# Squaring the last stage's keys on ScalarE instead of VectorE, in a two-layer attention and expert kernel on one core

## The reference, cut to what matters

```
xn = layernorm(x)
# attention, 16 heads of 8
q, k, v = split(xn @ w_qkv);  q = elu(q) + 1;  k = elu(k) + 1
y = (q @ (k^T v)) / (q @ sum(k))
# channel mix
x_prev = xn shifted by one token within its sequence
xr = mu_r * xn + (1 - mu_r) * x_prev
xk = mu_k * xn + (1 - mu_k) * x_prev
r = sigmoid(xr @ W_r^T)
k_act = square(relu(xk @ W_k^T))
x = x + (y @ w_proj + b_proj) + r * (k_act @ W_v^T)
```

## Time and profile before

| | |
|---|---|
| Three runs, median (lowest to highest) | 349.37 us (348.57 to 349.54) |
| The profiled execution, its own time | 349.86 us |
| Its span, first to last instruction | 348.1 us |
| Granted TensorE clock, mean | 0.995 of full speed |
| Busy in the span: PE, PEld, DVE, ACT, POOL | 95%, 84%, 92%, 80%, 65% |
| The last stage, from its first kv matmul to the end | 265.3 to 348.1 us |

### The profile page before, as it was taken

The page is one execution under the profiler, slowest core; times in us unless marked ns, Lnnn a source line. Parts: engine busy times, 40 slices in busy tenths (PEclk is TensorE's granted clock), DMA queues, the critical chain, the costliest instruction groups (busy, mean ns, idle before and its releaser), DMA issues.

```text
span 348.1 us, 9108 instructions
## 1 busy us (share of the span) xinstructions
PE 330.2 (95%) x2457; PEld 293.9 (84%) x2457; DVE 318.9 (92%) x590; ACT 278.4 (80%) x805; POOL 225.3 (65%) x238
## 2 busy tenths in 40 slices
PE   7999968889999999999999899999998999999995
PEld 3878424689999999999999899999997788778875
DVE  5899999989999999999899899999979799998665
ACT  2987956977899898889788778879997788777751
POOL 3799101876776688777777768777877278874110
PEclk9999989999999999999999999999999999999999
DMA  5785595334444555664655555676452002221012
GB/s 161 213 237 141 147 427 206 107 109 137 137 138 138 140 149 162 159 189 136 178 164 161 166 161 153 160 190 161 122 144 70 1 17 54 59 57 32 30 32 60
DMA packets 47120, 47.04 MB, mean 135 GB/s; under 512 B 8528, under 2 KB 35312, under 8 KB 46816
## 3 DMA queue, kind: packets, MB, share of 16 engines
q1 hardware_dynamic: 42032, 37.23, 35.4%
q0 software_dynamic: 4320, 8.86, 10.8%
q10 hardware_dynamic: 720, 0.38, 0.5%
HBM read 32.88 MB, written 13.50 MB: 133 GB/s over the span
## 4 chain that ended last, share of the span: by engine, by line
PE 78%; DVE 15%; DMA 2%; issue 2%; ACTq 1%; ACT 0%; SPq 0%; DVEq 0%
PE banks L575 17%; PE banks L587 17%; PE banks L783 5%; PE banks L784 5%; PE banks L1106 3%; PE banks L559 2%; PE banks L1182 2%; PE banks L1135 2%; PE banks L1164 2%; PE banks L1144 2%; PE banks L868 2%; PE banks L1116 2%; PE banks L1152 2%; DVE qk_exp L408 2%; PE banks L1171 2%
## 5 line engine op out<-in xcount | busy, mean ns | idle before, releaser
L503 POOL DMA_INDIRECT xg<-xn_rows,slot_tok x71 | 85.6, 1206 | 44.7 <-DVE slot_at L1819 23.0
L604 ACT ACTIVATE xT<-banks,b1T 128x128 f32<-128x128 f32 x284 | 81.8, 378 | 12.3 <-PE banks L575 11.9
L520 POOL DMA_INDIRECT qk_exp<-expert_rows,ranki x64 | 70.2, 1097 | 18.4 <-issue 17.1
L575 PE MATMUL banks<-xgT,w 128*128 128x128 f32 x568 | 75.5, 276 | 0.2 <-ACT xgT L596 0.2
L587 PE MATMUL banks<-w_sb,xT 128*128 x568 | 75.2, 275 | 0.1
L587 PEld LDWEIGHTS banks<-w_sb,xT 128*128 128x128 f32 x568 | 69.3, 192 | 0.9 <-issue 0.3
L575 PEld LDWEIGHTS banks<-xgT,w 128*128 128x128 f32 x568 | 69.0, 192 | 0.8 <-issue 0.7
L795 DVE TENSOR_TENSOR cq<-banks,phi 128x1152 f32<-128x1152 f32 x32 | 43.2, 1350 | 5.7 <-PE banks L784 5.7
L806 DVE TENSOR_REDUCE late<-cq 128x144 f32<-128x1152 f32 (+1 forms) x32 | 45.5, 1421 | 0.1
L696 ACT CAST high<-outer 128x1152 fp32r<-128x1152 f32 x32 | 37.0, 1156 | 6.8 <-DVE outer L685 5.0
L703 DVE TENSOR_TENSOR low<-outer,high 128x1152 fp32r<-128x1152 f32 (+1 forms) x32 | 38.7, 1210 | 1.5 <-ACT high L696 1.3
(11 more groups left out here) (224 smaller groups left out, 701.3 us busy)
## 6 DMA issues: line engine op xcount, KB each, us to landing
w<-in_L_ffn_W SPq DMA_DIRECT2D x71, 256.0 KB
expert_rows<-ye SPq DMA_DIRECT2D x71, 64.0 KB
expert_rows<-x_sb SPq DMA_DIRECT2D x2, 2048.0 KB, 9.8
x_sb<-in_L_attn_x SPq DMA_DIRECT2D x8, 256.0 KB, 4.5
xn_rows<-xn_all SPq DMA_DIRECT2D x8, 256.0 KB, 4.1
w_sb<-in_L_ffn_W SPq DMA_DIRECT2D x8, 256.0 KB, 4.5
out<-outer SPq DMA_DIRECT2D x7, 256.0 KB, 2.3
xg<-xn_rows,slot_tok POOLq DMA_INDIRECT x71
```

The lines of the kernel that those rows point to most:

```text
L503: pool.indirect_dma_start(out=xg[n][:, :], out_offset=None, in_=xn_dram, in_offset=bass.IndirectOffsetOnAxis(ap=slot_tok[:, j:j + 1], axis ...
L520: pool.indirect_dma_start(out=y_moe[:, i, k, :], out_offset=None, in_=y_dram, in_offset=bass.IndirectOffsetOnAxis(ap=ranki[:, 0, k, i:i + ...
L575: last = nc.tensor.matmul(slot_bank(j)[:, c * P:(c + 1) * P], w1[n][:, c * P:(c + 1) * P], xgT[p][:, :], start=True, stop=True)
L604: last = nc.scalar.activation(hidT[p][:, c, :], slot_bank(j)[:, c * P:(c + 1) * P], ACT.Gelu_apprx_tanh, bias=b1T[:, ds(e * NC + c, 1)])
```

## The change

The hunks are of `square_keys`, `last_scalar`, `last_vector`, `group_vector` and `group_scalar`, in this order. `square_keys` moves from VectorE's queue to ScalarE's, and becomes a Square of the activation functions in place of a product of two tensors. Its waits and its semaphore stay. On ScalarE it stands behind `gate_scalar` (the tanh) and ahead of `xT2_copy` in groups 0 to 6, and behind `yT1_copy` in group 7.

```
-    def square_keys(v, g):
-        v.wait_ge(relu_ready, g + 1)
-        if from_(g, 1):
-            v.wait_ge(vf_ps, g)
-        nc.vector.tensor_tensor(k_act, k_relu, k_relu, ALU.mult).then_inc(kact_ready, 1)
+    def square_keys(act, g):
+        act.wait_ge(relu_ready, g + 1)
+        if from_(g, 1):
+            act.wait_ge(vf_ps, g)
+        nc.scalar.activation(k_act, k_relu, ACT.Square).then_inc(kact_ready, 1)
...
@@ -1247,6 +1247,7 @@
         yT1_copy(act, g - 1)
+        square_keys(act, g)
         act.wait_ge(phik_ready, NG)
...
@@ -1258,7 +1259,6 @@
         phi_q_vector(v, g)
-        square_keys(v, g)
         v.wait_ge(nd_ps, g + 1)
...
```

## The result

The changed kernel takes 350.42 us in the median of 14 runs (350.08 to 352.74), the kernel before 349.24 us beside it (348.47 to 350.38). The ratio is 1.0041, with a 95% interval of 1.0028 to 1.0055: slower by 0.4%. The time lies in the predicted range and 0.1 us from the predicted 350.5; against the kernel before on the same chips it is 1.2 to 1.4 us more, where the sum said 1.1.

What follows compares the result with a forecast made beforehand. A loop through ScalarE, VectorE and TensorE was taken as the bound, with phi_k's wait binding groups 2 to 4. Delays 0.47 + 0.12 + 0.01 + 0.02 + 0.46 = +1.08 us gave a 350.5 us median, range 349.3 to 351.4.

Steps and rivals of the forecast that it cites:

- The loop, and where ScalarE's queue lies on it: Last stage: ScalarE's queue through mu, VectorE's mix to finish, TensorE's gates and keys, back to relu; sets 9.35 us a group.
- The price of a Square: ScalarE's queue: each 128x512 Square delays its successor 0.54 us, with bounds of 0.48 and 0.61.
- Group 0, +0.47; group 1, +0.12; groups 5 and 6, +0.23 each: Delay in us by group: phi_q waits for ScalarE in group 0; elsewhere the Square's 0.54 less slack before the yT1 copy.
- Groups 2 to 4, +0.03 together: Square's cost beyond the slack before the yT1 copy: +0.01, 0 and +0.02 us; removing the product counted as 0.
- worth nothing: Taking the 0.69 us products off VectorE gains 0 in groups 1 to 6, because mix waits for ScalarE's mu.
- the holes before KV: TensorE's waits for phi_k in groups 2 to 4, 0.76 us in all; a ceiling on the gain, taken as 0.
- phi_k's branch: Second branch of the loop, binding groups 2 to 4: KV_tensor waits for phi_k, 1.10 us beside GpSimd's add; length kept.
- Rival 1: VectorE's queue set groups 1 to 4 and is now free: -0.3 us, 349.1, at best -0.76; chance 0.10.
- Rival 2, absorption: Group 0's delay is taken back by slack in groups 2 to 4: about +0.5 us, 349.9; chance 0.12.
- Rival 3: Square costs its upper bound and TensorE's stall at the transposes adds 0.1 in six groups: 2.1 us, 351.5; chance 0.09.
- Rival 4: Square needs another function table, two 1.28 us loads in each of 7 groups: 18 us, 368.5; chance 0.03.
- Last group, hidden: Square behind the yT1 copy delays values_tensor, but its matmuls finish before the transposes can load: 0, at worst 0.1 us.

Runs made afterwards that it cites:

- e1: Square on ScalarE in group 0 only, VectorE's product kept in the other groups, against the kernel before; ratio 1.0013, stage +0.30 us.
- e2: Square on ScalarE in groups 5 and 6 only, VectorE's product kept elsewhere, against the kernel before; ratio 1.0023, stage +0.42 us.
- e4: The changed kernel with every Square run twice, the first into a spare tile; ratio to the kernel before 1.0124, stage 3.99 us longer than the changed kernel's.
- e3: The kernel before with the product dropped and nothing in its place, values made from the relu; ratio 0.9984, stage 0.78 us shorter.
- e9: The kernel before with VectorE's product reading the keys' PSUM bank as second operand instead of k_relu; ratio 0.9978, stage 0.73 us shorter.
- e12: The changed kernel with the Square behind the xT2 copy, finish at its old place; ratio to the kernel before 1.0029.
- e7: The kernel before with finish ahead of ffn and a group's moments behind the next group's phi_k on VectorE; ratio 1.0041.
- e8: The kernel before with finish ahead of ffn, moments behind the next phi_k, and the Square on ScalarE in groups 1 to 6; ratio 1.0008.
- e10: The kernel before with the product reading the keys' PSUM bank and finish ahead of ffn; ratio 0.9961, stage 1.01 us shorter.
- e11: The changed kernel with finish ahead of ffn and the Square behind the xT2 copy; ratio to the kernel before 1.0014.

## Why the prediction was right, point by point

- **The loop, and where ScalarE's queue lies on it.** Right, and shown: the cost appears in the groups into which the Square is put (e1, e2), and with no slack left a second Square costs its full 0.52 us (e4).
- **The price of a Square, 0.54 us to its successor.** It is 0.51 to 0.52. The Trainium skill's figure for immediate operands (ScalarE: Activation LUTs, What ACT_TABLE_LOAD costs) is an estimate of 0.52; e4's rows, 321.68 and 322.20, agree with it. (With 0.52 the prediction's sum comes to 0.97, not the 0.96 that it states.)
- **Group 0, +0.47; group 1, +0.12; groups 5 and 6, +0.23 each.** Measured 0.45, 0.13, 0.22, 0.24.
- **Groups 2 to 4, +0.03 together.** Measured -0.03, but that the two numbers are so close is luck. The step that says the product removed is "worth nothing" is the one that failed: taken off alone it is worth 0.78 us (e3), and the argument from mix being released by mu was no proof, since it followed VectorE's queue only, not what the product does to GpSimd: L303 0.32 us longer, the add late, phi_k 1.02 to 1.10 us instead of 0.66. In the changed kernel the holes before KV did close for the most part (phi_k 0.66 us in groups 2 and 4, 1.03 in group 3), but ScalarE's loop of 9.59 us had meanwhile become just as long as phi_k's branch was. Against the 9.34 to 9.41 us of e3, the Squares so cost 0.19 to 0.25 us in each of groups 2 to 6, and in groups 2 to 4 that took the place of the holes. The sum was right, this term's reason was not.
- **Rival 1** was nearer than its 0.10 suggests: its effect exists, though not its mechanism. e9 shows the gain with VectorE as busy as ever.
- **Rival 2, absorption:** out; the delay of group 0 stays in e1 but for 0.16 us, of which 0.09 is the phi_k of group 3.
- **Rival 3:** the Square costs 0.52, not its upper bound of 0.61; the stall at the transposes exists (TensorE's load of L1122 idles 0.17 us in the changed kernel), but doesn't add to the loop (e12). **Rival 4:** no table load behind 267.84.
- **Last group, hidden:** 12.04 us in both. The values' load waited 0.35 us for the Square, and the y1 transposes came right behind its eight loads. e4 shows how little cover was left: of the second Square's 0.52 us, 0.38 show.
- **The chances.** Slower by over 0.3% had 0.48, the same had 0.49, and the ratio is 1.0041 (from 1.0028). The sum of the stage, 1.01, would be 0.29%, on the other side of that line: which of the two it became was not foreseen. The rest of the measured difference, 0.2 to 0.4 us, lies within the scatter of the runs, and no row of the profiles accounts for it.

## What to carry to other kernels

Ask of an engine's queue not how busy it is but which loop through the engines it lies on, and how long it waits inside that stretch: 6.44 us busy of 9.35 left room for only 0.31 us more between the relu and the yT1 copy. Work moved to the emptier engine costs its full length, less that wait, once for every turn. And before moving an elementwise operation off VectorE, look at what it reads: taking one operand from PSUM brought what the move was after, at no cost to ScalarE.

## What the runs showed of the hardware

- A VectorE instruction with two SBUF tensors and a GpSimd instruction at the same time get in each other's way, and in each pair one alone pays. The product of 0.69 us stretched GpSimd's L303 from 1.02 to 1.04 us to 1.34 to 1.38 and kept its own length (before, e3, e9). GpSimd's add stretched phi_k from 0.66 to 1.03 and 1.10 and, when it fell wholly upon it, to 1.88, 2.14 and 2.22 us (e7, e8), and the product to 1.56 (e7, group 3); the add kept its 1.26 to 1.30 throughout. What is held up does not run on slowly but comes after the other: phi_k ends 0.55 to 0.57 us behind the add's end each time that it is stretched, L303 0.87 to 0.92 behind the product's. With one operand in PSUM the product did GpSimd no harm and was just as long (0.68).
- The Trainium skill, SBUF — State Buffer, section SBUF: two separate sides, has the port pair that the two share as an exclusive lock, also for a VectorE instruction with two SBUF inputs against a GpSimd one that reads SBUF: the one that starts first has it for its whole length, and the other is blocked. The rows agree on the blocking. On who is first they don't always: in e7 phi_k starts 0.30 and 0.38 us ahead of the add by the profile, and yet phi_k is the one held up.
- GpSimd's gathers (L520) take 0.94 us or up to 1.54 in the same kernel, by whether they start inside phi_q or mix. No run was made for this alone. So it is a matter of phase, as in group 3 of e10, whether the add meets phi_k.
- ScalarE's Square of 128x512 from SBUF to SBUF takes 0.63 us and lets the next start after 0.51 to 0.52 (behind the xT2 copy, in e11 and e12, 0.65 and 0.52 to 0.54); relu and tanh of the same size from PSUM take 0.60 and 0.59, and let it start after 0.47 to 0.50.
